# Query scratch loaded in four transfers, maxima turned in another bank, and the last batch's output products moved behind its loop

## What is computed

```python
qkv = hidden_states @ Wqkv            # q: 32 heads of 16; one k and one v of 16 for all heads
scores = jnp.einsum('bqhd,bkd->bhqk', q, k) * scale
scores = jnp.where(causal, scores + alibi, NEG_INF)
probs = jax.nn.softmax(scores, axis=-1)
attn = jnp.einsum('bhqk,bkd->bqhd', probs, v).reshape(B, S, H)
return attn @ Wo
```

## Time and profile before

| | |
|---|---|
| median of 3 runs | 447.17 us (444.88 to 447.2) |
| profiled execution | 446.26 us, span 444.2 us |
| PE, DVE, ACT, POOL busy | 89%, 58%, 40%, 40% of the span |
| first FFN, attention, second FFN | to about 130 us, 130 to 320 us, from 320 us |
| second loop, batches 0, 1, 2, 3 | from about 194, 216, 250, 283 us |

### The profile page before, as it was taken

One profiled execution on the slowest core, in us unless ns is written; L12 is line 12 of the kernel. 1 busy time (PEld: TensorE's weight loads), 2 busy tenths in 40 slices (PEclk: granted clock), 3 DMA queues, 4 the chain that ended last, 5 costly groups with the idle time before them and its releaser, 6 DMA issues.

```text
span 444.2 us, 8306 instructions
## 1 busy us (share of the span) xinstructions
PE 394.1 (89%) x2788; PEld 276.5 (62%) x2789; DVE 258.3 (58%) x638; ACT 177.3 (40%) x302; POOL 176.5 (40%) x268
## 2 busy tenths in 40 slices
PE   0799899999969998989979989889999879999972
PEld 0677578888646766555555555344687558888660
DVE  4579643332457975687775685466539933333357
ACT  1321246656202222157654464653340336665300
POOL 2431226666302772355544354452001055666300
PEclk9999999999998999999999999989999999999997
DMA  7999994544289468323133030010420043534278
GB/s 234 291 379 303 316 338 139 176 116 144 111 296 294 131 170 175 96 83 93 29 96 93 8 95 19 10 38 27 155 96 1 0 142 116 161 122 150 90 290 324
DMA packets 51052, 66.05 MB, mean 149 GB/s; under 512 B 8190, under 2 KB 30374, under 8 KB 50980
## 3 DMA queue, kind: packets, MB, share of 16 engines
q1 hardware_dynamic: 42652, 43.55, 31.1%
q0 software_dynamic: 6368, 19.32, 13.9%
q10 hardware_dynamic: 2000, 2.76, 2.0%
HBM read 46.32 MB, written 19.79 MB: 149 GB/s over the span
## 4 chain that ended last, share of the span: by engine, by line
PE 59%; DVE 16%; DMA 12%; SPq 6%; issue 4%; ACT 1%; POOL 1%; ACTq 0%; DVEq 0%; POOLq 0%
PE ps L1588 15%; PE ps L1595 7%; PE ps L1452 6%; PE ps L1738 6%; PE ps L1573 4%; SPq L394 4%; PE ps L1714 3%; PE ps L1657 3%; DMA turns<-in_L_ffn_sw_dram 3%; DMA q_dram<-arena 3%; PE ps L1686 3%; PE ps L1493 2%; DMA arena<-xn_dram,arena 2%; DVE arena L1264 2%; PE ps L1688 2%
## 5 line engine op out<-in xcount | busy, mean ns | idle before, releaser
L1264 DVE TENSOR_REDUCE arena<-ps 128x3 f32<-128x384 f32 x128 | 69.4, 555 | 33.7 <-PE ps L1688 31.6
L1588 PE MATMUL ps<-arena,wj 128*128 128x128 f32 x608 | 74.1, 274 | 0.0
L1588 PEld LDWEIGHTS ps<-arena,wj 128*128 128x128 f32 x608 | 71.0, 192 | 1.0 <-issue 1.0
L861 ACT ACTIVATE arena<-ps 128x768 f32<-128x768 f32 x64 | 51.2, 810 | 43.1 <-PE ps L1702 42.1
L647 POOL TENSOR_SCALAR_AFFINE_SELECT arena<-arena 128x512 f32<-128x512 f32 x64 | 40.7, 641 | 56.7 <-ACT arena L861 56.2
L1159 DVE SCALAR_TENSOR_TENSOR arena<-ps,arena 128x128 f32<-128x128 f32 x38 | 13.3, 351 | 80.1 <-ACT arena L753 80.1
L1452 PE MATMUL ps<-arena,turns 128*128 128x256 f32 x256 | 57.6, 381 | 0.6 <-DMA turns<-in_L_ffn_sw_dram 0.6
L1452 PEld LDWEIGHTS ps<-arena,turns 128*128 128x128 f32 x256 | 48.1, 190 | 9.0 <-issue 2.1
L553 POOL DMA_INDIRECT arena<-xn_dram,arena x34 | 33.2, 978 | 50.8 <-DVE arena L1099 25.2
L558 POOL DMA_INDIRECT y_dram<-arena x38 | 38.4, 1011 | 33.8 <-DVE arena L1166 25.5
L1686 PE MATMUL ps<-cb 128*128 128x256 bf16 x128 | 35.3, 276 | 5.2 <-DVE arena L1264 4.0
(11 more groups left out here) (196 smaller groups left out, 586.3 us busy)
## 6 DMA issues: line engine op xcount, KB each, us to landing
arena<-y_dram SPq DMA_DIRECT2D x16, 512.0 KB, 7.4
arena<-q_dram SPq DMA_DIRECT2D x36, 128.0 KB, 2.7
xn_dram<-arena SPq DMA_DIRECT2D x16, 256.0 KB, 5.3
w<-in_L_ffn_ew_dram SPq DMA_DIRECT2D x4, 1024.0 KB, 11.0
q_dram<-arena SPq DMA_DIRECT2D x16, 192.0 KB, 2.4
x<-_attn_hidden_states_dram SPq DMA_DIRECT2D x4, 512.0 KB, 6.2
out_dram<-x SPq DMA_DIRECT2D x8, 256.0 KB, 5.9
arena<-arena SPq DMA_DIRECT2D x30, 64.0 KB
```

The costliest lines, as they stand in the source:

```text
L861: act.activation(pr[:, n % 2, pair, :], ps[:, bank:bank + 2, :].rearrange("p a b -> p (a b)")[:, 0:768], ACT.Exp).then_inc(sem("exp"), 1)
L1264: dve.tensor_reduce(m3[:, h // (HEADS // 2), :, h % (HEADS // 2)], ps[:, bank, 0:3 * P].rearrange("p (n k) -> p n k", n=3), AX_X, ALU.max) ...
L1588: ins = pe.matmul(o, wj[:, par, c, n * INTER:(n + 1) * INTER], xgT[:, par, c, :], start=(c == 0), stop=(c == KC - 1))
```

## The change

Three edits. **Scratch:** `q_dram` and `k_dram` get another order. A load of half the heads (for batch 1 of all) is four DMAs, one of 48 rows (all three query parts, against key part 0) and three of 16 rows; `k_dram` is stored in three DMAs as before, the first with key part 0 repeated three times. **Maxima:** they are turned into columns 256 to 383 of `PS_O`, ahead of the round's `weigh`, and the waits that `PS_A` needed go; the next `weigh` waits for ACT's copy. **Order:** at the end of a batch SP issues `q_rows` ahead of `odd_in`. In the last batch both `inverse_rows` stand in round 5, in two banks, instead of rounds 3 and 4; batch 2's output products stand in round 7 (two of eight) and behind the last `weigh` (six), instead of rounds 5 and 6; DVE's and ACT's work is reordered with them.

```diff
@@ -50,12 +50,10 @@
-QPART = (0, 0, 0, 1, 1, 2)
-KPART = (0, 1, 2, 0, 1, 0)
+QPART = (0, 0, 1)
 STEP = 16
 STEPS = P // STEP - 1
-SPREAD = len(QPART)
-R_REST = SPREAD * HD
+R_REST = 2 * 3 * HD
 R_MAX = R_REST + 6 + QT * STEPS
@@ -128,8 +126,8 @@
         y_dram = nc.dram_tensor("y_dram", (ROWS_Y, DIM), F32).ap()
-        q_dram = nc.dram_tensor("q_dram", (BATCH, 3, DIM, SEQ), BF16).ap()
-        k_dram = nc.dram_tensor("k_dram", (BATCH, HD, len(KPART), SEQ), BF16).ap()
+        q_dram = nc.dram_tensor("q_dram", (BATCH, HEADS, HD, 3, SEQ), BF16).ap()
+        k_dram = nc.dram_tensor("k_dram", (BATCH, 2, HD, 3, SEQ), BF16).ap()
         m_dram = nc.dram_tensor("m_dram", (2, 3, 2, HEADS, P), BF16).ap()
...
@@ -308,13 +306,16 @@
-        def m_bank(b, half):
-            return PS_S if (b, half) == (0, 0) else PS_A
+        def turned(b, half):
+            return ps[0:HEADS, PS_S, 0:P] if (b, half) == (0, 0) else ps[0:HEADS, PS_O, SEQ:SEQ + P]
+        def inverse_bank(b, half):
+            return PS_S if (b + 2, half) == (BATCH, 1) else PS_A
-        Q_INS = (16 * (len(QPART) + 1), 16 * len(QPART))
+        Q_INS = (16 * (2 + len(QPART)), 16 * (1 + len(QPART)))
...
@@ -378,10 +379,11 @@
                     if c is None:
-                        for at, count in K_RUNS:
-                            sp.dma_start(k_dram[b, :, at:at + count], kp[:, 0:count]).then_inc(sem("k_out"), 16)
+                        sp.dma_start(k_dram[b, 0], kp[:, 0:1].to_broadcast([HD, 3, SEQ])).then_inc(sem("k_out"), 16)
+                        sp.dma_start(k_dram[b, 1, :, 0:2], kp[:, 1:3]).then_inc(sem("k_out"), 16)
+                        sp.dma_start(k_dram[b, 1, :, 2], kp[:, 1]).then_inc(sem("k_out"), 16)
                     else:
-                        sp.dma_start(q_dram[b, :, c * P:(c + 1) * P, :].rearrange("k p t -> p k t"), qp[:, :, c, :]).then_inc(sem(f"q_out{c}"), 16)
+                        sp.dma_start(q_dram[b, c * 8:(c + 1) * 8].rearrange("h d k t -> (h d) k t"), qp[:, :, c, :]).then_inc(sem(f"q_out{c}"), 16)
@@ -390,12 +392,14 @@
                     sp.wait_ge(sem("st_done"), HEADS // 2 * (b - 2) + last // 2)
-                for r in range(len(QPART)):
-                    sp.dma_start(qside[r:R_REST:SPREAD, p, first:last],
-                                 q_dram[b, QPART[r], first * HD:last * HD].rearrange("(h d) t -> d h t", d=HD)
+                sp.dma_start(qside[0:3 * HD, p, first:last], q_dram[b, first:last].rearrange("h d k t -> (d k) h t")
+                             ).then_inc(sem(f"q_in{p}{0 if first == 0 else 1}"), 16)
+                for r in range(3):
+                    sp.dma_start(qside[3 * HD + r:R_REST:3, p, first:last],
+                                 q_dram[b, first:last, :, QPART[r]].rearrange("h d t -> d h t")
                                  ).then_inc(sem(f"q_in{p}{0 if first == 0 else 1}"), 16)
                 if first == 0:
-                    sp.wait_ge(sem("k_out"), 16 * len(K_RUNS) * (b + 1))
+                    sp.wait_ge(sem("k_out"), 16 * K_STORES * (b + 1))
                     k_rows(sp, b)
...
@@ -457,9 +461,9 @@
                 sums_of_even(4 * b + 3)
-                odd_in(4 * b + 3)
                 if b + 2 < BATCH:
                     q_rows(b + 2, HEADS // 2, HEADS)
+                odd_in(4 * b + 3)
                 if b + 1 < BATCH:
...
@@ -883,9 +887,8 @@
                         inverse_high(b - 1)
-            xnT_copy(1, 0)
             outputs(8 * BATCH - 1)
-            for t in range(1, 4):
+            for t in range(4):
                 xnT_copy(1, t)
@@ -1297,7 +1300,7 @@
                 two = aT[b % 2][:, 2 * half:2 * half + 2].rearrange("p c t -> p (c t)")
-                dve.tensor_tensor(two, ps[:, PS_A, :], two, ALU.mult).then_inc(sem("normed"), 1)
+                dve.tensor_tensor(two, ps[:, inverse_bank(b, half), :], two, ALU.mult).then_inc(sem("normed"), 1)
@@ -1307,7 +1310,7 @@
                 dve.wait_ge(sem("a_rec"), c + 1)
-                dve.tensor_tensor(aT[b % 2][:, c, :], aT[b % 2][:, c, :], s, ALU.mult).then_inc(sem("normed"), 1)
+                dve.tensor_tensor(aT[b % 2][:, c, :], aT[b % 2][:, c, :], s, ALU.mult).then_inc(sem("normed_last"), 1)
@@ -1383,12 +1386,6 @@
                         residual(b - 1, 0)
-                    if q == 4 and not more:
-                        normalise(b - 1, 1)
-                    if q in (5, 7) and not more:
-                        normalise_last(q // 2 - 2)
-                    if q == 6 and not more:
-                        residual(b - 1, 0)
                     if q == 0 and b >= 2:
@@ -1396,29 +1393,39 @@
                         invert_half(b - 1, 0)
-                    if q == 3 and not more:
-                        normalise(b - 1, 0)
                     if q == 4 and b >= 1 and more:
                         normalise(b - 1, 1)
-                    if q == 7 and b >= 1:
+                    if q == 7 and b >= 1 and more:
                         row_stats(QT * (b - 1))
                         ln_stats(1, b - 2)
-                    if b + 1 == BATCH and q in (3, 4, 5, 6):
+                    if not more:
                         if q == 3:
                             dve.wait_ge(sem("st_done"), HEADS // 2 * b)
-                        ln_rows(1, q - 3)
-                    if b + 1 == BATCH and q == 7:
-                        residual(b - 1, 1)
-                        row_stats(QT * (b - 1) + 1)
-                        ln_stats(1, b - 1)
-            normalise_last(KC - 2)
+                            ln_rows(1, 0)
+                            normalise_last(0)
+                        if q == 4:
+                            ln_rows(1, 1)
+                        if q == 5:
+                            normalise(b - 1, 0)
+                            normalise(b - 1, 1)
+                        if q == 6:
+                            ln_rows(1, 2)
+                            ln_rows(1, 3)
+                            normalise_last(1)
+                        if q == 7:
+                            residual(b - 1, 0)
+                            row_stats(QT * (b - 1))
+                            normalise_last(2)
+                            residual(b - 1, 1)
+                            row_stats(QT * (b - 1) + 1)
+                            ln_stats(1, b - 1)
+            normalise_last(KC - 1)
             ln_rows(1, 4)
             ln_rows(1, 5)
-            normalise_last(KC - 1)
             for t in range(QT):
@@ -1702,12 +1709,21 @@
-            def weigh(n):
+            behind = [0]
+            def weigh(n, turn=None):
                 b = n // 8
-                pe.wait_ge(sem("sel"), 2 * n + 2)
                 if n >= 1:
                     pe.wait_ge(sem("oT"), n)
+                if turn is not None:
+                    pe.wait_ge(sem("m_copy"), 2 * turn[0] + turn[1])
+                    max_turn(*turn)
+                    behind[0] = 2 * turn[0] + turn[1] + 1
+                elif behind[0]:
+                    pe.wait_ge(sem("m_copy"), behind[0])
+                    behind[0] = 0
+                pe.wait_ge(sem("sel"), 2 * n + 2)
                 for k in range(QT):
@@ -1718,23 +1734,27 @@
                 pe.wait_ge(sem("m_nm"), 2 * b + half + 1)
-                pe.transpose(ps[0:HEADS, m_bank(b, half), 0:P], m3[:, half, 0:QT].rearrange("p t h -> p (t h)"), ident).then_inc(sem("m_t"), 1)
+                pe.transpose(turned(b, half), m3[:, half, 0:QT].rearrange("p t h -> p (t h)"), ident).then_inc(sem("m_t"), 1)
                 pe.wait_ge(sem("inverse"), b + 1)
-                pe.wait_ge(sem("m_copy"), min(2 * b + 4 + half, 2 * BATCH))
-                if half == 1:
+                if b >= 1:
+                    pe.wait_ge(sem("att_x"), QT * b)
+                if half == 1 and inverse_bank(b, 1) == PS_A:
                     pe.wait_ge(sem("normed"), 2 * b + 1)
                     for k in range(3):
-                        ins = pe.matmul(ps[:, PS_A, c % 2 * SEQ:(c % 2 + 1) * SEQ], cb[:, B_SEL + c * P:B_SEL + (c + 1) * P], inverse[:, k],
+                        ins = pe.matmul(ps[:, inverse_bank(b, half), c % 2 * SEQ:(c % 2 + 1) * SEQ], cb[:, B_SEL + c * P:B_SEL + (c + 1) * P], inverse[:, k],
                                         start=(k == 0), stop=(k == 2))
-                pe.wait_ge(sem("normed"), 2 * b + 2 if b + 1 < BATCH else 2 * b + c + 1)
+                if b + 1 < BATCH:
+                    pe.wait_ge(sem("normed"), 2 * b + 2)
+                else:
+                    pe.wait_ge(sem("normed_last"), c + 1)
                 ins = pe.matmul(ps[:, at_bank(b, t), :], aT[b % 2][:, c, t * P:(t + 1) * P], wo[:, c, :], start=(c == 0), stop=(c == KC - 1))
@@ -1789,8 +1809,10 @@
                         scores(b + 1, 4 * q + 1, PS_S + 1)
-                    if q in (3, 4) and not more:
-                        inverse_rows(b - 1, q - 3)
+                    if q == 5 and not more:
```

(55 more changed lines are left out.)

## The result

The changed kernel takes 448.69 us (median of 13 runs, 446.20 to 450.15) against 446.10 (13 runs, 443.41 to 449.73): ratio 1.0061, interval 1.0034 to 1.0088. It is slower by 0.6%, where 440.4 was forecast. Its profiled execution took 449.69 us (span 447.6), 3.4 more than that of before.

What follows compares the result with a forecast made beforehand. PE was taken as the bound, mostly dense in the attention with a few nameable stops. Terms 1.3 + 1.6 + 1.1 + 2.4 = 6.4 us, from 446.26 to 439.9, forecast as 440.4; range 436.2 to 445.6.

Steps and rivals of the forecast that it cites:

- Scratch, 1.3 forecast: Early query loads and stores: two fewer DMA issues per load shrink PE's stops at 170.45 and 181.76, gaining 1.3 us.
- The second is set by the drain of 1572 KB, 199 GB/s in the row at 176 us: PE's stop at 181.76: batch 1's load still drains in 7.9 us but starts 1.3 earlier; the stop shrinks by 0.3.
- All of it starts 1.3 us earlier: SP's early list of loads and stores moves 1.3 us ahead, so PE's first stop of 0.96 us goes.
- ACT waiting for the scratch stores as long as before: Sign listed as showing the forecast wrong: ACT's early waits for stores, 4.45 us each, do not shorten.
- The slower rival: Early load and batch 1: heads' parts 12 KB apart in DRAM halve the load rate; 6.5 us slower, 453.3, chance 0.06.
- The loads ahead of `odd_in`, 1.2 forecast: Batch 1: the maxima are stored earlier, PE's 1.85 us stop goes, less 0.4 for late sums and 0.2 for the inverse.
- it stands 0 to 1.0 us: Batch 1: DVE's wait for sums queued behind 786 KB of loads; 0.5 us taken, of which 0.4 reaches PE.
- Maxima and inverse: Batches 1 and 2: turning maxima ahead of `weigh` gains 0.4 us each; the inverse, next late, costs 0.2 each.
- Batch 2: Gain of 1.1 us: 0.7 from the 0.89 us reload wait, less the inverse, and 0.4 from the maxima.
- Last batch, 2.4 forecast: From batch 2's end to `shared_up`: ACT-paced rounds of 1.88 us, then dense PE work, ending 2.4 us earlier.
- 5.9 us of stops and slow clock: Last batch before the change: PE work sums to 31.1 of 37.0 us; the remaining 5.9 are stops and slow clock.
- the clock falls in the new loop: Last batch: slow-clock rounds of 2.75 us take the 2.4 back; 4.0 gained in all, 442.8, chance 0.12.

Runs made afterwards that it cites:

- `e_spread_scratch_only`: The kernel before with only the scratch edit, in four loads whose rows are spread over all 96 instead of packed; ratio 0.9951.

## Why the prediction was wrong

- **Scratch, 1.3 forecast, -3.9 in the trace.** The step that failed first is "The second is set by the drain of 1572 KB, 199 GB/s in the row at 176 us": the 199 was read from transfers whose 16 rows lie six apart, and was carried to transfers that write other rows. Half of the bytes went at 130 to 148. The query store behind them landed 5.61 us after its issue at 175.81, 1.2 later than before by the time of the profile and 2.5 later counted from the first query product, although the forecast had it 1.3 earlier. PE's stops grew by 2.5 us (2.48 + 1.98 for 0.96 + 0.98); the other 1.4 I put down to the stretch at 1.2 GHz behind them. The issues did become fewer, but not all cheap (1.58 and 1.71 us for the last two).
- **The same term, a second step:** "All of it starts 1.3 us earlier", so that the first stop goes. The keys' stores were all issued by 163.07, before only by 166.60, yet ACT's wait for them ended at 168.94, before at 168.78. The waits stay even where the rate is the old one: 4.59 and 4.47 us in `e_spread_scratch_only`, and with spread rows the early stretch takes 57.4 to 58.6 us, 57.8 before. The issues saved ahead of these stores bought nothing; the forecast's own sign, "ACT waiting for the scratch stores as long as before", came.
- **The slower rival, 0.06.** "The rearranged load drains slowly" named the right place with a wrong cause (distance in DRAM) and a swing for both halves of the bytes; six loads in the new order drain at the old rate. Its argument against, "pieces are 512 bytes as before, and neighbours in DRAM", is true and says nothing of the side that is written.
- **The loads ahead of `odd_in`, 1.2 forecast.** The step that failed is "it stands 0 to 1.0 us", of which 0.5 was taken for DVE and 0.4 for PE: measured were 2.75 and 2.99. So the sum named the stop and had it 2.3 and 2.6 us too short. With spread rows it is still 2.03 for DVE. There the load is issued from 217.08, moves 72 GB/s in 218 to 219 and 266 in 219 to 220, and is through between 222 and 223; the sums, whose second DMA is issued at 220.35, land 3.31 us later, while DVE asks at 221.75. The forecast had the start-up (1.2 us, the load under way from 218.4) and the drain (through at 222.3) right for these rows. It had the sums land by 222.2 to 223.1, right behind the drain; they landed at 223.66, and DVE asked 0.3 earlier than the 222.09 of before. The slow rows add the last 0.7. The rule of the Trainium skill that the prediction weighed (DMA: Bandwidth & Descriptors, "Queues, rings and completion order"), that a small late transfer waits for all before it on its ring, is what the traces show: 4.17 us for `odd_in` behind 786 KB, and a stop of 0.59 us once half of the bytes stand behind it. In some traces the clock then fell too (batch 1 took 17.87 and 18.57 us).
- **Maxima and inverse.** As forecast, in the trace: no wait of `max_turn`, no wait for the reload in round 4, 0.23 and 0.19 for the inverse. Batch 2 gave 1.0 for 1.1.
- **Last batch, 2.4 forecast, 2.1 measured.** But that the size fits is in part luck, since it rests on the clock: in the old order it fell in three of five traces (46.1 to 47.7 us), in the other two the stretch took 44.8, against 44.3 to 44.5 in twelve traces of the new one. Without a fall the edit is worth 0.3 to 0.55. The forecast's 5.9 us of stops and slow clock named the fall, but took it for certain.
- **The rival "the clock falls in the new loop"** didn't come there, but the clock did fall elsewhere: behind the early stops, which no case of mine had. (Its 2.75 us for a round at 1.2 GHz should have been twice the 1.45, 2.9; it changes nothing.)
- **The range** ended at 445.6, since all of its cases but the one at 0.06 kept the drain of before, and none the fall of the clock behind the early stops.

## What to carry to other kernels

A rate read from one transfer holds only for transfers that write the same partitions: before rows are regrouped to save issues, look at a window of a load into such rows, and try the same load with the rows spread; fewer and wider DMAs into a packed range can be slower than many into a spread one. And ask what a DMA waits for behind its issue: the stores that queue behind a load here were issued earlier and landed no earlier. When a load is moved ahead of a small transfer on one queue, price the small one as start-up (here over 1 us) plus the whole drain plus its own landing, and try putting half of the load behind it. A stop's price includes the clock that it may drop, and one trace may have such a fall by chance: compare medians, or several traces.

## What the runs showed of the hardware

- Loads in 512-byte pieces into partitions 0 to 47 ran at 101 to 148 GB/s, whether 16 or 48 rows wide, those into 48 to 95 or spread over 0 to 95 at about 200 (single windows from 169), at equal busy share (1.2 in this view) of the DMA engines.
- The clock fell behind the early stops of PE in the six traces in which the two together were longest (3.49 to 5.30 us), and in one more behind the first, of 2.36 us; it did not in the ten in which they were 1.53 to 2.73 us together. With the fall the early stretch takes 60.9 to 63.7 us, without it 57.4 to 58.6. In batch 1 stops near 3 us dropped it in some traces and not in others.
- The second FFN, equal in all these kernels, took from 114.1 to 117.8 us behind the logits: 114.1 with 6.3 us of it at 1.2 GHz in the trace of before, 117.8 with 15.4 us in that of after. So one profile against another can be off by 3 us where the medians are not: here 3.4 against 2.6.
